# Four steps of a key-blocked attention at other places in the orders of ScalarE, VectorE and the DMA queue

## What is computed

```python
def _L0_xattn_ref(x, context, ln_gamma, ln_beta, w_q, w_kv, w_out, b_out, gate):
    xn = _layernorm(x, ln_gamma, ln_beta)
    q = (xn @ w_q).reshape(B, SQ, NUM_HEADS, DIM_HEAD)
    k, v = jnp.split(context @ w_kv, 2, axis=-1)
    ...
    scores = jnp.einsum('bqhd,bkhd->bhqk', q * SCALE, k)
    attn = jax.nn.softmax(scores, axis=-1)
    out = jnp.einsum('bhqk,bkhd->bqhd', attn, v).reshape(B, SQ, INNER)
    out = out @ w_out + b_out
    return out * jnp.tanh(gate[0])
```

## Time and profile before

| | us |
|---|---|
| median of 3 runs | 4263.38 |
| lowest, highest | 4258.98, 4272.05 |
| the profiled execution | 4275.2 |
| its span, from the first to the last instruction | 4273.4 |

### The profile page before, as it was taken

The page is one execution under the profiler, slowest core; times in us unless marked ns, Lnnn a source line. Parts: engine busy times, 40 slices in busy tenths (PEclk is TensorE's granted clock), DMA queues, the critical chain, the costliest instruction groups (busy, mean ns, idle before and its releaser), DMA issues. The chain is left out here.

```text
span 4273.4 us, 80912 instructions
## 1 busy us (share of the span) xinstructions
PE 3694.9 (86%) x30262; PEld 2624.8 (61%) x30262; DVE 2503.5 (59%) x3308; ACT 2307.2 (54%) x4294; POOL 1639.5 (38%) x1365
## 2 busy tenths in 40 slices
PE   5899999999999999999867797689999987667399
PEld 3677777777777777777644696545555543333298
DVE  5555555555555555555336412378788777458577
ACT  3566666666666656666614211256666666535165
POOL 2566666666666666666703200301110100014033
PEclk9899999999999999999978898789999999879599
DMA  6666666666666666666220374788788744100011
GB/s 226 252 230 227 242 247 231 242 239 226 242 242 233 241 233 227 224 225 220 92 82 9 123 270 176 238 181 166 178 176 170 165 81 67 26 16 1 12 50 43
DMA packets 231714, 723.26 MB, mean 169 GB/s; under 512 B 47372, under 2 KB 128524, under 8 KB 162444
## 3 DMA queue, kind: packets, MB, share of 16 engines
q1 hardware_dynamic: 228640, 709.70, 53.0%
q0 software_dynamic: 2688, 8.39, 0.5%
HBM read 623.61 MB, written 94.37 MB: 168 GB/s over the span
## 5 line engine op out<-in xcount | busy, mean ns | idle before, releaser
L753 POOL TENSOR_TENSOR wa_acc<-wa_acc,wa_probs 128x512 f32<-128x512 f32 x960 | 1234.9, 1286 | 610.0 <-ACT wa_probs L616 499.4
L680 DVE TENSOR_REDUCE wa_mx<-wa_ps_m 128x2 f32<-128x1024 f32 x512 | 627.4, 1225 | 449.7 <-PE wa_ps_m L488 449.6
L616 ACT ACTIVATE wa_probs<-wa_ps_s 128x512 f32<-128x512 f32 x1024 | 531.4, 602 | 618.2 <-PE wa_ps_s L530 614.1
L1292 DVE TENSOR_REDUCE na_mx<-na_ps_m 128x2 f32<-128x1024 f32 x512 | 613.9, 1220 | 202.7 <-PE na_ps_m L1113 199.1
L1237 ACT ACTIVATE na_probs<-na_ps_s 128x512 f32<-128x512 f32 x1024 | 556.0, 594 | 315.7 <-PE na_ps_s L1133 313.3
L608 ACT ACTIVATE wa_ps_s<-wa_m_wide 128x512 f32<-128x512 f32 x1024 | 575.5, 602 | 1.0
L509 PE MATMUL wa_ps_o<-wa_probs,wa_values 128*64 128x256 f32 x4096 | 499.5, 386 | 1.0 <-ACT wa_probs L616 1.0
L452 PE MATMUL wa_ps_k<-wa_k_ctx,wa_w_k 128*128 128x512 f32 x1488 | 425.8, 422 | 0.0
L475 PE MATMUL wa_ps_m<-wa_w_v,wa_v_ctx 128*128 128x256 f32 x2880 | 379.8, 283 | 1.3 <-DVE wa_mx L680 1.3
L475 PEld LDWEIGHTS wa_ps_m<-wa_w_v,wa_v_ctx 128*128 128x128 f32 x2880 | 359.9, 190 | 28.4 <-DVE wa_mx L680 14.5
L509 PEld LDWEIGHTS wa_ps_o<-wa_probs,wa_values 128*64 128x64 f32 x4096 | 271.7, 137 | 155.4 <-issue 14.0
(11 more groups left out here) (344 smaller groups left out, 5855.4 us busy)
## 6 DMA issues: line engine op xcount, KB each, us to landing
wa_k_ctx<-ctx_split SPq DMA_DIRECT2D x248, 1024.0 KB, 4.9
wa_v_ctx<-ctx_split SPq DMA_DIRECT2D x120, 1024.0 KB, 6.9
na_ctx<-ctx_split SPq DMA_DIRECT2D x56, 1024.0 KB, 11.4
na_keys<-k_rows SPq DMA_DIRECT2D x384, 128.0 KB
ctx_split<-wa_stage SPq DMA_DIRECT2D x32, 1024.0 KB, 3.9
wa_land<-in_ctxT SPq DMA_DIRECT2D x32, 512.0 KB, 7.9
ge_w_b<-in_w_rows SPq DMA_DIRECT2D x8, 2048.0 KB, 7.8
k_rows<-na_k_high SPq DMA_DIRECT2D x64, 256.0 KB, 2.8
```

The costliest lines, as they stand in the source:

```text
L616: act.activation(probs[:, c % R:c % R + 2, h * SQ:(h + 1) * SQ], ps_s[n % BANKS][:, :].rearrange("p (c n) -> p c n", c=2), ACT.Exp).then_i ...
L680: dve.tensor_reduce(mx[:, half, :, k], ps_m[:, :, :], AX.X, ALU.max).then_inc(m_taken, 1)
L753: pool.tensor_tensor(to[:, :], to[:, :], probs[:, c % R, :], ALU.add).then_inc(summed, 1)
L1292: dve.tensor_reduce(mx[:, half, :, k], ps_m[n % 2][:, :, :], AX.X, ALU.max).then_inc(m_taken, 1)
```

## The change

Four pieces move. Nothing is added to the computation; one wait is added.

- ACT: `split` from the end of stage 2 to the end of stage 1.
- DVE: `copy_out` from ahead of the first maximum to between the two. `divide` is cut in two. `invert`, the reciprocal, goes to the end of stage 1, behind the keys and values, with a new wait that the multiplication of the group before is done. `multiply` goes to the end of stage 3. `finish_maximum` goes from the head of stage 7 to the end of stage 6.
- SP: `store` of stage 3 goes ahead of that stage's `key_context` and `value_context`.

```diff
@@ sync
             for j in range(-2, LAST):
                 a, st = j // SS, j % SS
+                if j >= 0 and st == 3 and a < BLOCKS - CG:
+                    store(a + CG)
                 kb = key_block(j - 1)
...
                 if j >= 0 and st == 1 and 3 <= a + 2 < G:
                     queries(a + 2)
-                if j >= 0 and st == 3 and a < BLOCKS - CG:
-                    store(a + CG)
@@ scalar
-                if j >= 0 and st == 2 and a < BLOCKS - CG:
+                if j >= 0 and st == 1 and a < BLOCKS - CG:
                     split(a + CG)
@@ vector
-            def divide(a):
+            def invert(a):
                 dve.wait_ge(o_copied, a + 1)
+                if a:
+                    dve.wait_ge(o_ready, a)
                 dve.reciprocal(rden[:, :], o_raw[:, SQ:2 * SQ]).then_inc(rden_ready, 1)
+
+            def multiply(a):
                 dve.wait_ge(rden_ready, a + 1)
...
-            for j in range(-2, LAST + 2):
+            for j in range(-2, LAST + 4):
                 a, st = j // SS, j % SS
                 of_max, kb = max_block(j), key_block(j)
-                if st == SS - 1 and a + 1 < G:
-                    finish_maximum(a + 1)
+                if of_max is not None:
+                    take_maximum(*of_max, 0)
                 if st == 1 and j > 1:
                     copy_out(a - 1)
                 if of_max is not None:
-                    take_maximum(*of_max, 0)
                     take_maximum(*of_max, 1)
-                if st == 1 and j > 1:
-                    divide(a - 1)
                 if j >= 0 and st == 2 and a < BLOCKS - CG:
                     split_low(a + CG)
                 if kb is not None:
                     take_keys(kb)
                 for n, (q, hb) in enumerate(value_units(j)):
                     take_values(q, hb, ps_m[:, n, :])
+                if st == 1 and j > 1:
+                    invert(a - 1)
+                if st == 3 and j > 3:
+                    multiply(a - 1)
+                if st == SS - 2 and a + 1 < G:
+                    finish_maximum(a + 1)
```

## The result

| | before | changed |
|---|---|---|
| median, us | 4267.72 (4 runs) | 4161.30 (4 runs) |
| lowest, highest | 4258.98, 4283.38 | 4153.45, 4167.73 |
| ratio, 95% interval | | 0.9746, 0.9711 to 0.9781 |
| span of the profiled execution | 4273.4 | 4165.9 |

What follows compares the result with a forecast made beforehand. The prediction took PE, waiting for DVE where it stands still, as the bound. Split 83.4, group 0 3.6 and copy with division 15.2 made 102.2 us off the median 4263.4: 4161.2 us, range 4146 to 4180.

Steps and rivals of the forecast that it cites:

- The bound: Attention: PE bounds, and where it stands still it waits for DVE, which idles 3.49 us for ACT's part of the split.
- the distance of the copies: Starts of the stage 1 copy, groups 1 to 23 against groups without a split: the split costs 83.4 us.
- Group 0: It has a split but lies outside groups 1 to 23; moving ACT's split gives another 3.6 us there.
- DVE's part beside POOL: Stage 2: DVE's split waits for a POOL addition's end, finishing 4.8 (even) or 6.2 us (odd) in; no PE wait.
- The rival with missed turns: Stage 2: DVE's split misses turns between POOL's additions, 14 us of the gain go, 4175 us; chance 0.12.
- the other two of the faster side: All DVE waits vanish, odd groups' reciprocal fits: 4150 us, chance 0.07; split stays late, ACT waiting in stage 1: 4248, 0.03.
- The division: Copy and reciprocal in stage 1: saves 0.71 us per even and 0.3 per odd group, 15.2 us over groups 1 to 30.
- DVE's hand-over behind the reciprocal: Odd groups, stage 1 into 2: reciprocal from 5.28 to 7.05 us, second maximum 2.58 us into stage 2, 0.66 late.
- Multiplication, final maximum, store: Multiplication at stage 3's end hidden, final maximum nothing, SP's early store delays a key load 1 to 2 us: no cost.
- Sum: Whole kernel: 83.4 + 3.6 + 15.2 = 102.2 us gained, giving 4161.2 us against the median.

## Why the prediction was right

*The bound.* PE waiting for DVE, and DVE for ACT's split, was the right reading: with the split alone moved, 87.4 us came where 87.0 were forecast for it (83.4 + 3.6). The step that carried this was to price it by the distance of the copies and not by the waits. The waits of the split in groups 1 to 23, 12 x 2.33 + 11 x about 3.0, sum to 61 us; the other 22 us are the slow clock behind them: 17 falls of 1.2 to 1.3 us make 21 to 22, and PE's busy time fell by 22.6 us. Group 0 was put at 3.6 us; the part ahead of group 1 is 4.3 us shorter, which proves little, as the start varies by some 5 us between executions.

*DVE's part beside POOL.* The odd group's split was to end 6.2 us into stage 2 and did (1053.59 - 1047.39), and the even one takes 1.22 us. The rival with missed turns did not occur. Nor did the other two of the faster side: DVE does not wait for ACT's split any more, and one DVE wait stayed in the odd groups.

*The division.* Forecast 15.2 us, measured 16.7 us beyond the run with the split alone, and 1.18 x 15 = 17.7 us by the pair of groups without a split (120.58 before, 119.40 after). The even groups won 0.80 us, not 0.71: their stage 2 had started later than its wait of 0.59 us says, by 0.67 us in the distances of PE's maxima (6.00 us from the second maximum of stage 1 to stage 2 before, 5.33 after). The odd groups won 0.40, not 0.30: 0.51 us of waiting stayed where 0.66 were forecast. The mis-sized term is DVE's hand-over behind the reciprocal. I had put 1.77 us between its start and the next instruction's; it was 1.66, and the first maximum behind it took 1.16 instead of 1.23 us, so the second one came 2.43 us into stage 2 and not 2.58. The term was too small by 1.5 to 2.5 us. The mechanism, a gap that is too short for the reciprocal in the short stage, is shown by the run that moved it.

*Multiplication, final maximum, store.* Hidden, as forecast. The multiplication took 1.03 and 0.75 us in groups 16 and 15, below the 1.28 counted, and no wait of PE follows it; that it met POOL's additions at another point is likely but was not tested. The store's place costs no time. The prediction saw the key block as just fitting, with landing times of 4.9 us; a load beside the store took 6.8 us or more, and yet at least 2.2 us were left.

*Sum.* Middle 101.1, start 4.3, rest 2.1 us, together 107.5 of the span against 102.2 forecast. Split and division make 101.1 in the middle where 83.4 + 15.2 = 98.6 were forecast. The 2.1 us of the rest belong to no step of the change.

## What to carry to other kernels

With orders written by hand, price a misplaced step by the period of the loop with and without it, where the program holds both; the sum of the waits misses what follows a wait. Look for the producer that sits at the end of its stage while its consumer stands in the middle of the same one: one stage earlier costs nothing if the input is there. And before a step is put into a gap, compare the gap in the shortest stage, not in the typical one: the reciprocal of 1.74 us fits the long stages and not the short, and putting it where all stages are long gave 9.4 us more, about 8 of them by the wait that went. A step hidden today can still use up slack: the early store cost no time and brought the key loads some 2 us closer to being late.

## What the runs showed of the hardware

Around the end of waits of PE of 2.33 to 3.28 us the granted clock fell to its lower level, 1.2 GHz, in 17 of groups 1 to 23 of the kernel before, and stayed at 2.4 GHz in the other six, at equal waits. With waits of at most 0.8 us, as in the run with the split alone, it was 1.00 in every one of groups 1 to 29. One fall lengthened a group by 1.2 to 1.3 us. DVE's two-input split waited for the end of a POOL addition and took 2.09 us instead of 1.22, and the addition beside it took 2.08 us instead of 1.28, even though both had slack enough here that PE never felt it. A key load of 1 MB landed in 7.8 us beside the store of the same size and in 4.7 us behind it.
